# Transposing layer A's normalised rows: from a host-transposed input to one DMA crossbar transfer per group

## The chip, the cores and the metric

The kernel runs on one NeuronCore of a Trainium2 chip. The metric is device time in microseconds (us), from the first to the last instruction and what lies around them. An engine is named PE (TensorE matmul), PEld (TensorE weight load), DVE (VectorE), ACT (ScalarE), POOL (GpSimd) or SP (SyncE, which here issues nearly all DMAs).

## The reference

Input `x` holds 128 graphs of 128 tokens with 384 features, `adj` a 128 x 128 matrix for each. Two layers follow each other, each on layer-normalised rows and each with a residual.

```
x = x + gnn(layernorm(x), adj, adj, Wq, Wk, Wv, bv, Wo, bo)
x = x + ffn(layernorm(x), Wqk, bqk, Wv, bv, conv_w, conv_b, glob, ...)
...
q = (x @ Wq.T).reshape(b, n, 12, 32)          # gnn: layer A
k = (x @ Wk.T).reshape(b, n, 12, 32)
v = (x @ Wv.T + bv).reshape(b, n, 12, 32)
scores = einsum('bqhd,bkhd->bhqk', q, k) * scale + 2 * adj
out = einsum('bhqk,bkhd->bqhd', softmax(scores), v) @ Wo.T + bo
```

Layer A is attention with 12 heads and an additive bias. Layer B (`ffn`) is a causal attention with three experts of width 128, one of which has a convolved query, and a top-2 gate. The change touches layer A alone, and in it the step from `layernorm(x)` to the operand of the products with Wq, Wk and Wv.

## The kernel before, in words

The 128 batches are worked in 32 groups of four (`GB = 4`, `NG = 32`). The matmuls of q, k and v need the normalised rows transposed: features on the partitions, in three chunks of 128 (`KC = 3`), and tokens along the row. They are also wanted in two fp16 parts, a high part and a rest (`a_hT_hi`, `a_hT_lo`), so that three fp16 matmuls (`three_pass`) stand for one fp32 matmul.

The work is cut into steps with names such as `A.qk.0`, and each engine goes through its own written-out list of steps in order: `FIRST_STEPS` (groups 0 and 1), `ORDER_OF_STEPS` (one turn, repeated for 30 turns with groups 2 to 31) and `LAST_STEPS`. In turn t the steps marked `ahead` (`A.hT`, `A.qk`, `A.stack`) work on group t, the other A steps on group t-1 and the B steps on group t-2. An engine that waits in one step holds up all steps behind it in its list. The steps that matter here, for a turn:

- PE: `... B.qk.3 A.mix.0 A.turn.1.0 A.turn.1.1 B.qk.4 B.qk.5 A.score.3.0 B.v.3 A.score.3.1 A.turn.1.2 A.proj.0 A.qk.0 A.mix.1 ...`. `A.qk.0` is the first to read the transposed rows. Each `A.qk` is nine matmuls of 512 columns.
- POOL: `... A.norm.1 A.hx.0 A.hx.1 A.hx.2 A.norm.2 ...`. `A.hx.c` adds the negative mean to chunk c of the transposed x (line 1177).
- DVE: `... A.score.2.2 A.hm.0 B.v.2 A.hm.1 A.hm.2 A.hT.0 A.mix.0 A.smax.2 A.hT.1 A.hT.2 B.v.3 ...`. `A.hm.c` multiplies chunk c by 1/std (line 966), `A.hT.c` writes the low part (line 971).
- ACT: `... A.turn.1.0 A.hT.0 A.mix.0 A.hT.1 A.turn.1.1 A.hT.2 B.qk.4 A.score.2.1 B.qk.5 ...`. `A.hT.c` writes the high part (line 709).
- SP: `A.stat A.rows A.xT A.stack.0 A.res A.adj A.stack.1 B.proj.0 ...`. `A.stat` stores a group's means and 1/std to DRAM, `A.rows` loads them back broadcast over all partitions (`stat_wide`), `A.xT` loads the next group's x, which the host has laid out transposed (`xt`). `A.stack.0` and `A.stack.1` then copy q and k within SBUF in 12 transfers of 96 KB each, for the scores of the next turn.

Groups 0 and 1 do without the host-transposed input. There POOL (and DVE for two batches of group 0, the step `W.share`) normalises rows token-major (`h1`), PE transposes them through PSUM (line 589), and ACT and DVE split what lies in PSUM.

Of the kernel before, what the change touches and what calls it, by code (L numbers as in the profile page):

```python
# [35 lines left out]
P = 128  # L36
# [17 lines left out]
H1_POOL = 2  # L54
# [34 lines left out]
        A.hT.0@0 W.turn.0@0 W.spread.0@0 A.hT.1@0 A.hT.2@0 W.warm.1@0 A.qk.0@0 A.qk.1@0 W.turn.1@0 A.qk.2@0  # L89
        A.qk.3@0 W.spread.1@0 A.qk.4@0 A.qk.5@0 W.turn.2@0 A.v.0@0 W.spread.2@0 W.warm.0@0 A.score.0.0@0  # L90
        A.score.0.1@0 A.score.0.2@0 A.v.1@0 A.v.2@0 A.score.1.0@0 A.score.1.1@0 A.v.3@0 A.hT.0@1 A.score.1.2@0
        A.turn.0.0@0 A.turn.0.1@0 A.score.2.0@0 A.hT.1@1 A.hT.2@1 A.turn.0.2@0 A.score.2.1@0 A.score.2.2@0
        A.qk.0@1 A.mix.0@0 A.turn.1.0@0 A.qk.1@1 A.turn.1.1@0 A.score.3.0@0 A.score.3.1@0 A.turn.1.2@0 A.qk.2@1
        A.score.3.2@0 A.qk.3@1 A.mix.1@0 A.turn.2.0@0 A.qk.4@1 A.turn.2.1@0 A.qk.5@1 A.turn.2.2@0 A.proj.0@0
        A.proj.1@0 A.mix.2@0 A.turn.3.0@0 A.turn.3.1@0 A.turn.3.2@0 A.proj.2@0 A.mix.3@0 A.proj.3@0
    """,
    "act": """
        A.hT.0@0 W.hi.0@0 A.hT.1@0 W.hi.1@0 A.hT.2@0 W.sum.5@0 W.sum.4@0 A.qk.0@0 A.qk.1@0 W.sum.3@0 A.qk.2@0
        A.qk.3@0 W.sum.6@0 A.qk.4@0 A.qk.5@0 W.hi.2@0 W.stack.1@0 A.score.0.0@0 A.score.0.1@0 A.score.0.2@0
        W.hi.3@0 A.hT.0@1 A.score.1.0@0 W.hi.4@0 A.score.1.1@0 A.score.1.2@0 A.hT.1@1 A.turn.0.0@0 W.hi.5@0  # L100
        A.turn.0.1@0 A.hT.2@1 A.score.2.0@0 A.turn.0.2@0 W.hi.6@0 A.score.2.1@0 A.mix.0@0 A.qk.0@1 A.turn.1.0@0
        A.qk.1@1 A.turn.1.1@0 W.hi.7@0 A.turn.1.2@0 A.score.2.2@0 A.qk.2@1 A.score.3.0@0 A.score.3.1@0 A.mix.1@0
        A.qk.3@1 A.turn.2.0@0 A.qk.4@1 A.score.3.2@0 A.turn.2.1@0 A.turn.2.2@0 A.qk.5@1 A.mix.2@0 A.turn.3.0@0
# [42 lines left out]
        A.score.2.2 A.hm.0 B.v.2 A.hm.1 A.hm.2 A.hT.0 A.mix.0 A.smax.2 A.hT.1 A.hT.2 B.v.3 A.score.3.0 A.proj.0  # L146
        A.norm.2 A.score.3.1 A.qk.0 A.mix.1 B.gate.0 B.score.0 A.qk.1 A.score.3.2 B.gate.1 B.score.1 B.gate.2
        B.norm.0 A.qk.2 B.norm.1 A.smax.3 A.norm.3 B.score.2 A.qk.3 B.mix.0 A.proj.1 B.norm.2 B.score.3 B.mix.1
        B.proj.0 A.qk.4 A.mix.2 A.qk.5 B.norm.3 B.proj.1 A.ln2.0 B.mix.2 A.ln2.1 A.proj.2 A.mix.3 A.ln2.2
        B.mix.3 B.proj.2 A.proj.3 A.ln2.3 B.proj.3  # L150
    """,
    "pool": """
        A.res.0 A.ln1 A.res.1 B.res.0 B.res.1 A.norm.0 A.res.2 A.res.3 A.norm.1 A.hx.0 A.hx.1 A.hx.2 A.norm.2
        B.norm.0 B.norm.1 B.res.2 A.norm.3 B.norm.2 B.norm.3 A.ln2.0 B.res.3 A.ln2.1 A.ln2.2 A.ln2.3 A.adj
    """,
    "sp": """
        A.stat A.rows A.xT A.stack.0 A.res A.adj A.stack.1 B.proj.0 B.proj.1 B.proj.2 B.proj.3
# [52 lines left out]
def turned(step, g):  # L210

    return step[:2] == ("A", "hT") and g >= TURNED

# [8 lines left out]
def ahead(step):  # L222
    return step[0] == "A" and step[1] in ("hT", "qk", "stack", "xT", "stat", "rows", "hx", "hm")
# [20 lines left out]
TURNED = 2  # L244
# [11 lines left out]
def build(nc, x, xT, stat_rows, adj, wq, wk, wv, wo, a_bv, a_bo, wqk, bqk, wv2, wg1, wp, b_bv, bg1, wg2, bg2, b_bp,  # L256
          conv_w, conv_b, out):
    with ExitStack() as ctx:
# [178 lines left out]
        def following(g):  # L437
            return g + 1
# [27 lines left out]
        def _(sp):  # L466
# [68 lines left out]
        def _(pe):  # L535
# [17 lines left out]
            def do(step, g, last):  # L553
# [676 lines left out]
```

## Time and profile before

| what | value |
|---|---|
| time, median of 3 runs | 2218.86 us (2217.16 to 2220.27) |
| span of the profiled execution | 2214.1 us |
| what lies around the span, by the median | 4.8 us |
| PE busy | 2167.0 us, 98% |
| DVE busy | 1959.1 us, 88% |
| ACT busy | 1490.3 us, 67% |
| POOL busy | 1198.7 us, 54% |
| mean granted TensorE clock | 0.997 |

The profiled execution has no time of its own beside its span; the median stands for it. Shares of busy time are means over the whole span. Whether a wait costs anything is seen only in the stretch where it lies, so most of the rows further down come from one turn in the middle, between 985 and 1075 us.

### The profile page before, as it was taken

How to read it: one execution, taken by the hardware profiler on the slowest of the kernel's cores; microseconds unless marked ns; L12 is line 12 of the kernel's file. 1: busy time of each engine (PE TensorE's matmuls, PEld its weight loads, DVE VectorE, ACT ScalarE, POOL GpSimd, SP SyncE). 2: the span in 40 equal slices, each digit the busy share in tenths (PEclk: the TensorE clock that was granted, in tenths of full speed). 3: DMA queues.
4: the chain of work that ended last, by engine and by line, in shares of the span. 5: the costliest groups of instructions: out<-in, count | busy, mean ns of one | idle time of the engine just before them, and what ended most of it. 6: DMA issues, size and time to landing. Idle time of an engine off the chain costs nothing.

```text
span 2214.1 us, 51113 instructions
## 1 busy us (share of the span) xinstructions
PE 2167.0 (98%) x16581; PEld 1388.2 (63%) x16581; DVE 1959.1 (88%) x7242; ACT 1490.3 (67%) x5298; POOL 1198.7 (54%) x1521
## 2 busy tenths in 40 slices
PE   5899999999999999999999999999999999999988
PEld 3566666666666666666666666666666666666655
DVE  6889998889988899988899988899988899888984
ACT  4667766677666676666676666677666776666763
POOL 2755565555565545565545665555655555655452
PEclk9999999999999999999999999999999999999999
DMA  5332333332333332333322333322333323333200
GB/s 178 77 93 54 80 90 98 92 84 55 88 87 101 92 77 58 92 87 92 100 69 59 100 87 92 99 52 75 94 94 92 83 59 86 87 101 92 47 27 29
DMA packets 182105, 182.62 MB, mean 82 GB/s; under 512 B 48977, under 2 KB 173521, under 8 KB 181841
## 3 DMA queue, kind: packets, MB, share of 16 engines
q1 hardware_dynamic: 179648, 178.07, 31.1%
q8 instruction: 134, 2.20, 0.5%
q14 instruction: 131, 1.07, 0.3%
q10 hardware_dynamic: 2192, 1.29, 0.2%
HBM read 78.50 MB, written 25.29 MB: 47 GB/s over the span
## 4 chain that ended last, share of the span: by engine, by line
PE 93%; DVE 3%; SPq 1%; ACT 1%; DMA 1%; issue 1%; POOL 0%; DVEq 0%
PE B_bank L546 33%; PE A_bank L546 32%; PE A_bank L626 7%; PE A_bank L638 4%; PE B_bank L620 4%; PE B_bank L645 4%; PE A_bank L613 4%; PE B_bank L630 2%; PE B_bank L589 2%; DVE raw_score L1001 1%; SPq L521 1%; DMA x1res<-in_wqk 1%; DVE smax L1007 0%; DVE V L990 0%; ACT S L755 0%
## 5 line engine op out<-in xcount | busy, mean ns | idle before, releaser
L1147 POOL TENSOR_TENSOR S<-S,rowf 128x512 f32<-128x512 f32 x384 | 414.9, 1108 | 459.9 <-DVE rowf L1026 457.1
L748 ACT ACTIVATE S<-raw_score,smin 128x128 f32<-128x128 f32 x1536 | 595.0, 392 | 94.6 <-DVE smin L1001 94.6
L1001 DVE CUSTOM_DVE_ANT_0 raw_score<-A_bank,adj,s_unit 128x128 f32<-128x128 f32 x1536 | 433.1, 344 | 6.5 <-PE A_bank L613 3.4
L1152 POOL TENSOR_TENSOR S<-S,row2f 128x384 f32<-128x384 f32 x128 | 105.8, 826 | 450.2 <-DVE row2f L1034 447.2
L748 ACT ACTIVATION_READ_ACCUMULATOR S<-raw_score,smin 128x1 f32 x1536 | 293.4, 191 | 0.0
L626 PE MATMUL A_bank<-ident,S 128*128 128x128 f32 x1536 | 218.7, 275 | 5.9 <-POOL S L1147 5.2
L1007 DVE TENSOR_REDUCE smax<-raw_score 128x12 f32<-128x1536 f32 x128 | 222.7, 1740 | 0.0
L762 ACT ACTIVATE PT<-A_bank 128x512 f32<-128x512 f32 x384 | 210.0, 590 | 7.6 <-PE A_bank L626 6.9
L626 PEld LDWEIGHTS A_bank<-ident,S 128*128 128x128 f32 x1536 | 176.5, 141 | 33.2 <-issue 10.4
L713 ACT ACTIVATE b_hT_hi<-B_bank 128x512 f16<-128x512 f32 x96 | 53.2, 588 | 191.1 <-PE B_bank L589 191.1
L762 ACT ACTIVATE PT<-B_bank 128x384 f32<-128x384 f32 x128 | 62.8, 491 | 158.9 <-PE B_bank L630 158.9
L755 ACT ACTIVATE S<-S,s2min 128x128 f32<-128x128 f32 x384 | 148.3, 389 | 3.4 <-DVE s2min L1011 3.4
L613 PE MATMUL A_bank<-Ks,Qs 96*128 96x128 f16 x1536 | 133.5, 219 | 5.6 <-DMA Ks<-k_hi 2.7
L1011 DVE CUSTOM_DVE_ANT_0 S<-B_bank,later 128x128 f32<-128x128 f32 x384 | 90.6, 286 | 53.1 <-PE B_bank L620 52.9
L613 PEld LDWEIGHTS A_bank<-Ks,Qs 96*128 96x128 f16 x1536 | 110.0, 97 | 39.0 <-issue 3.9
L546 PE MATMUL A_bank<-wv_hi,a_hT_hi 128*128 128x384 f16 x384 | 125.7, 327 | 5.9 <-issue 4.9
L546 PE MATMUL B_bank<-wv2g_hi,b_hT_hi 128*128 128x416 f16 x384 | 130.3, 339 | 0.0
L546 PE MATMUL B_bank<-wv2g_hi,b_hT_lo 128*128 128x416 f16 x384 | 130.1, 339 | 0.0
L546 PE MATMUL B_bank<-wv2g_lo,b_hT_hi 128*128 128x416 f16 x384 | 130.1, 339 | 0.0
L546 PE MATMUL A_bank<-wo_hi,oT_hi 128*128 128x384 f16 x384 | 125.2, 326 | 2.6 <-DVE oT_lo L982 2.6
L1133 POOL TENSOR_TENSOR xres<-xin,bo_row 128x384 f32<-128x384 f32 x128 | 127.6, 1008 | 0.0
L546 PE MATMUL B_bank<-wp_hi,yT_hi 128*128 128x384 f16 x384 | 125.5, 327 | 1.3 <-DVE yT_lo L982 1.3
(196 smaller groups left out, 6330.0 us busy)
## 6 DMA issues: line engine op xcount, KB each, us to landing
xin<-in_x SPq DMA_DIRECT2D x32, 768.0 KB, 5.0
Qs<-q_hi SPq DMA_DIRECT2D x256, 96.0 KB, 2.2
out<-x1res SPq DMA_DIRECT2D x128, 192.0 KB, 2.1
Ks<-k_hi SPq DMA_DIRECT2D x252, 96.0 KB, 3.2
xt<-in_xT SPq DMA_DIRECT2D x30, 768.0 KB, 4.2
stat_wide<-stat_rows SPq DMA_DIRECT2D x30, 512.0 KB, 4.4
Qs<-q_lo SPq DMA_DIRECT2D x128, 96.0 KB, 2.2
Ks<-k_lo SPq DMA_DIRECT2D x126, 96.0 KB, 2.9
```

Of the source, the lines that this page charges most:

```text
L546: mm = nc.tensor.matmul(dst, left(c)[a], right(c)[b], start=(c == 0 and n == 0), stop=(c == KC - 1 and n == 2))
L613: mm = nc.tensor.matmul(dst[:, tok(j)], Qs[:, c * HPC + j, tok(b)], Ks[:, c * HPC + j, tok(b)], start=True, stop=True)
L626: mm = nc.tensor.transpose(dst[:, tok(j)], S[b % 2][:, c * HPC + j, :], ident[:])
L748: ins = nc.scalar.activation(S[b % 2][:, h, :], raw_score[:, h, :], ACT.Exp, bias=smin[b % 2][:, h:h + 1], scale=-1.0, accum_out=ssum[b % ...
L755: ins = nc.scalar.activation(S2[b % 2][:, e, :], S2[b % 2][:, e, :], ACT.Exp, bias=s2min[b % 2][:, e:e + 1], scale=-1.0, accum_out=s2sum[b ...
L762: nc.scalar.activation(dst, src[:, 0:dst.shape[1]], ACT.Copy).then_inc(evacuated[stage, "act"], 1)
L1001: ins = nc.vector.tensor_tensor_reduce(raw_score[:, h, :], src[:, j * T:(j + 1) * T], adj2[:, b, :], s_unit[:], 3.0e38, ALU.add, ALU.min, ...
L1007: nc.vector.tensor_reduce(smax[b % 2][:], raw_score[:], AXX, ALU.max).then_inc(maxed, 1)
L1011: ins = nc.vector.tensor_tensor_reduce(S2[b % 2][:, e, :], src[:, e * T:(e + 1) * T], later[:], 1.0, 3.0e38, ALU.add, ALU.min, s2min[b % 2 ...
L1133: nc.gpsimd.tensor_tensor(xres[:, b, :], xin[g % 2][:, b, :], bo_row[:], ALU.add).then_inc(xres_ready, 1)
L1147: nc.gpsimd.tensor_tensor(S[b % 2][:, hs, :], S[b % 2][:, hs, :], rowf[b % 2][:, hs].unsqueeze(2).broadcast_to([P, HPC, T]), ALU.mult).the ...
L1152: nc.gpsimd.tensor_tensor(S2[b % 2][:], S2[b % 2][:], row2f[b % 2][:].unsqueeze(2).broadcast_to([P, NE, T]), ALU.mult).then_inc(normed2, 1)
```

## The change

The host-transposed input `xT`, the DRAM scratch `stat_rows` and the steps `A.stat`, `A.rows`, `A.xT`, `A.hx`, `A.hm` and `W.share` are gone. For every group POOL now normalises each of the four batches token-major (`A.h1.0` to `A.h1.3`, through two buffers of one batch each), ACT and DVE split each batch into its fp16 parts (`A.hT.0` to `A.hT.3`, 128 x 384 each), and SP, once all four batches are split, issues one transposing DMA from `h1_parts` (128 partitions x 3072 fp16, 768 KB) to `h1T`, which holds 24 blocks of 128 x 128. PE's `A.qk.0` waits for the whole transfer. PE's transposes of groups 0 and 1 are gone too. The lists of PE for a steady turn are unchanged; ACT and DVE get a fourth `A.hT` right behind the third.

```diff
-        A.score.2.2 A.hm.0 B.v.2 A.hm.1 A.hm.2 A.hT.0 A.mix.0 A.smax.2 A.hT.1 A.hT.2 B.v.3 A.score.3.0 A.proj.0
...
+        A.score.2.2 B.v.2 A.hT.0 A.mix.0 A.smax.2 A.hT.1 A.hT.2 A.hT.3 B.v.3 A.score.3.0 A.proj.0 A.norm.2
...
-        A.res.0 A.ln1 A.res.1 B.res.0 B.res.1 A.norm.0 A.res.2 A.res.3 A.norm.1 A.hx.0 A.hx.1 A.hx.2 A.norm.2
...
+        A.res.0 A.ln1 A.res.1 B.res.0 B.res.1 A.norm.0 A.res.2 A.res.3 A.norm.1 A.h1.0 A.h1.1 A.h1.2 A.h1.3
...
-        A.stat A.rows A.xT A.stack.0 A.res A.adj A.stack.1 B.proj.0 B.proj.1 B.proj.2 B.proj.3
+        A.hT.0 A.hT.1 A.hT.2 A.hT.3 A.stack.0 A.res A.adj A.stack.1 B.proj.0 B.proj.1 B.proj.2 B.proj.3
...
-        xt = sb("xt", [P, KC, GB * T])
-        h1 = xt[:].rearrange("p c n -> p (c n)").rearrange("p (b n) -> p b n", b=GB)
+        h1 = sb("h1", [P, 2, C])
+        h1_parts = sb("h1_parts", [P, GB, 2, C], F16)
+        h1T = sb("h1T", [P, GB, 2 * KC, T], F16)
...
+                if (stage, kind) == ("A", "hT"):
+
+                    wait_evacuated(sp, step, g)
+                    if b == GB - 1:
+                        if not g == 0:
+                            wait_products(sp, ("A", "v", GB - 1, 0), before(g))
+                            wait_products(sp, ("A", "qk", 2 * KC - 1, 0), before(g))
+                        sp.dma_start_transpose(h1T[:].rearrange("p b n t -> p (b n) t"),
+                                               h1_parts[:].rearrange("p b n c -> p (b n c)")).then_inc(h1_turned, 16)
...
+                if A and kind == "qk" and b == 0:
+                    pe.wait_ge(h1_turned, count(g, 16, 16))
+
+                def columns(c):
+                    return [h1T[:, :, n + c, :] for n in (0, KC)] if A else [h[:, c, :] for h in (hT_hi, hT_lo)]
...
+                    act.wait_ge(h1_ready, count(g, GB, b + 1))
+                    if b == 0 and not g == 0:
+                        act.wait_ge(h1_turned, count(g, 16, 0))
+                    nc.scalar.activation(h1_parts[:, b, 0, :], h1[:, b % 2, :], ACT.Copy, scale=H_SCALE)\
                         .then_inc(hi_ready["ahead"], 1)
...
-            def normed_rows1(g):
+            def normed_rows1(g, b):
                 pool.wait_ge(rstd1_done, count(g, 1, 1))
...
+                if b >= 2:
+                    wait_evacuated(pool, ("A", "hT", b - 2, 0), g)
+                elif not g == 0:
+                    wait_evacuated(pool, ("A", "hT", b + 2, 0), before(g))
+                nc.gpsimd.tensor_scalar(h1[:, b % 2, :], xin[g % 2][:, b, :], stat[g % 2][:, 0, b:b + 1],
+                                        stat[g % 2][:, 1, b:b + 1], ALU.add, ALU.mult).then_inc(h1_ready, 1)
```

The operand that PE streams in `A.qk` was one run of 512 columns and is now four runs of 128 (`columns`).

## Rows read from the trace of the kernel before

**Rows 1.** The page: busy time of each engine.

```profile
PE 2167.0 (98%) x16581; PEld 1388.2 (63%) x16581; DVE 1959.1 (88%) x7242; ACT 1490.3 (67%) x5298; POOL 1198.7 (54%) x1521
```

**Rows 2.** Windows, one turn: length, busy of PE, PEld, DVE, ACT, POOL; clock, DMA.

```profile
1000.00:1067.00 67.00, 67.00 (x519) 43.04 (x517) 60.57 (x226) 45.94 (x166) 37.07 (x47) 1.00 0.33 84
```

**Rows 3.** The chain that ended last, in order of time: start, length, what.

```profile
472.22 9.24 PE A_bank L546 x45
...
1074.93 9.23 PE A_bank L546 x45
```

**Rows 4.** Waits of PE over the span: total, times, longest.

```profile
PE A_bank L546 <- DVE a_hT_lo L971: 2.2, 1, 2.2
```

**Rows 5.** Timeline of a turn, 990 to 1000.1 us: start, length, engine, line.

```profile
990.26 4.19 POOL L1177 TENSOR_TENSOR xt<-xt,stat_wide 128x512 f32<-128x512 f32 x3
...
991.58 1.74 DVE L966 TENSOR_TENSOR xt<-xt,stat_wide 128x512 f32<-128x512 f32 x1
992.00 0.60 ACT L762 ACTIVATE PT<-A_bank 128x512 f32<-128x512 f32 x1 [0.17 <-PE A_bank L626]
...
993.24 0.64 DVE L990 SCALAR_TENSOR_TENSOR V<-B_bank,v_unit,bvg_row 128x416 f32<-128x416 f32 x1
...
993.89 0.47 ACT L766 ACTIVATE oT_hi<-A_bank 128x384 f16<-128x384 f32 x1
...
995.57 0.58 ACT L762 ACTIVATE PT<-A_bank 128x512 f32<-128x512 f32 x1
...
996.13 0.54 DVE L982 TENSOR_TENSOR oT_lo<-A_bank,oT_hi 128x384 f16<-128x384 f32 x1
...
996.60 1.74 DVE L1007 TENSOR_REDUCE smax<-raw_score 128x12 f32<-128x1536 f32 x1
...
998.26 1.28 DVE L971 SCALAR_TENSOR_TENSOR a_hT_lo<-xt,a_hT_hi 128x512 f16<-128x512 f32 x2
...
1000.06 0.38 PE L546 MATMUL A_bank<-a_hT_hi,wq_hi 128*128 128x512 f16 x1
```

**Rows 6.** Groups of instructions: count, busy us and mean ns, idle before.

```profile
L1177 POOL TENSOR_TENSOR xt<-xt,stat_wide 128x512 f32<-128x512 f32 x90 | 126.0, 1427 | 0.0
...
L966 DVE TENSOR_TENSOR xt<-xt,stat_wide 128x512 f32<-128x512 f32 x90 | 106.3, 1207 | 0.0
...
L1165 POOL TENSOR_SCALAR h<-x,nmean,rstd 128x384 f32<-128x384 f32 x128 | 84.6, 661 | 14.0
...
L971 DVE SCALAR_TENSOR_TENSOR a_hT_lo<-xt,a_hT_hi 128x512 f16<-128x512 f32 x90 | 58.6, 677 | 0.0
...
L709 ACT ACTIVATE a_hT_hi<-xt 128x512 f16<-128x512 f32 x90 | 56.4, 627 | 47.2 <-DVE xt L966 47.2
```

**Rows 7.** DMA issues: count, KB each, median us from issue to landing.

```profile
Qs<-q_hi SPq DMA_DIRECT2D x256, 96.0 KB, 2.2
...
xt<-in_xT SPq DMA_DIRECT2D x30, 768.0 KB, 4.2
```

**Rows 8.** SP's own queue in a turn: start, length, what it issued.

```profile
1015.12 5.13 SPq L521 DMA_DIRECT2D Qs<-q_hi  x8
```

**Rows 9.** A long gap of PE at the start (timeline), then windows with the clock.

```profile
33.84 0.27 PE L565 MATMUL B_bank<-ident,wmax 128*2 128x128 f32 x1
39.03 0.39 PE L546 MATMUL A_bank<-wv_hi,a_hT_hi 128*128 128x384 f16 x1 [4.91 <-issue]
...
40.00:42.00 2.00, 2.00 (x8) 0.68 (x6) 1.83 (x8) 0.00 (x0) 1.82 (x3) 0.50 1.13 239
42.00:44.00 2.00, 2.00 (x16) 1.98 (x17) 1.01 (x5) 0.00 (x0) 1.91 (x4) 0.86 0.35 67
```

**Rows 10.** Timeline of groups 0 and 1: low parts, first `A.qk`.

```profile
19.52 1.88 DVE L971 SCALAR_TENSOR_TENSOR a_hT_lo<-A_bank,a_hT_hi 128x512 f16<-128x512 f32 x3
20.35 0.38 PE L546 MATMUL A_bank<-a_hT_hi,wq_hi 128*128 128x512 f16 x1 [2.22 <-DVE a_hT_lo L971]
...
64.61 0.63 PE L546 MATMUL A_bank<-a_hT_hi,wq_hi 128*128 128x512 f16 x1
```

More of the change, by code:

```diff
@@ L53 @@
 GH = 32
-H1_POOL = 2
 VG = C + GH
@@ L96 @@
+        A.turn.0.2@0 A.score.2.1@0 A.score.2.2@0 A.qk.0@1 A.mix.0@0 A.turn.1.0@0 A.qk.1@1 A.turn.1.1@0
+        A.score.3.0@0 A.score.3.1@0 A.turn.1.2@0 A.qk.2@1 A.score.3.2@0 A.qk.3@1 A.mix.1@0 A.turn.2.0@0 A.qk.4@1
+        A.turn.2.1@0 A.qk.5@1 A.turn.2.2@0 A.proj.0@0 A.proj.1@0 A.mix.2@0 A.turn.3.0@0 A.turn.3.1@0
+        A.turn.3.2@0 A.proj.2@0 A.mix.3@0 A.proj.3@0
     """,
     "act": """
-        A.hT.0@0 W.hi.0@0 A.hT.1@0 W.hi.1@0 A.hT.2@0 W.sum.5@0 W.sum.4@0 A.qk.0@0 A.qk.1@0 W.sum.3@0 A.qk.2@0
@@ L99 @@
[L99 to L103, printed above, removed]
@@ L206, with crossed @@
 }
-def turned(step, g):
-    return step[:2] == ("A", "hT") and g >= TURNED
+def crossed(step):
+    return step[:2] == ("A", "hT")
 def parse(word):
@@ L222, in ahead @@
 def ahead(step):
-    return step[0] == "A" and step[1] in ("hT", "qk", "stack", "xT", "stat", "rows", "hx", "hm")
+    return step[0] == "A" and step[1] in ("hT", "qk", "stack", "h1")
 def whole_program(engine):
@@ L691, in do @@
                 A = stage == "A"
-                src = bank_of(step, g) if kind in EVAC and not turned(step, g) else None
+                src = bank_of(step, g) if kind in EVAC and not crossed(step) else None
                 if kind == "hi":
@@ L703, in do @@
                                           k_parts[n % 2][j * HD:(j + 1) * HD, :, :]).then_inc(ks_stacked, 16)
[L704 to L709 removed]
+                elif kind == "hT" and A:
+                    act.wait_ge(h1_ready, count(g, GB, b + 1))
+                    if b == 0 and not g == 0:
+                        act.wait_ge(h1_turned, count(g, 16, 0))
+                    nc.scalar.activation(h1_parts[:, b, 0, :], h1[:, b % 2, :], ACT.Copy, scale=H_SCALE)\
                         .then_inc(hi_ready["ahead"], 1)
@@ L943, in do @@
                 A = stage == "A"
-                src = bank_of(step, g) if kind in EVAC and not turned(step, g) else None
+                src = bank_of(step, g) if kind in EVAC and not crossed(step) else None
                 freed = evacuated[counted(step), "dve"] if stage != "W" else None
@@ L950, in do @@
                         weight_max(b)
-                    elif kind == "share":
-                        h_share()
                     elif kind == "top":
@@ L1117, in _ @@
             statistics1(0)
-            normed_rows1(0)
+            for b in range(GB):
+                normed_rows1(0, b)
             pool.wait_ge(bo_loaded, 16)
```

156 lines of the change are left out of this document (52 added, 104 removed).

## The prediction

> **What bounds the kernel now.** I read the page first. It puts PE at 2167.0 us, 98% of the span, with DVE next at 88% [rows 1]. A share of busy time can hide stretches with other limits, so next come the windows: in a turn of the middle PE is busy for all of its 67.00 us, at full clock, while DVE has 6.4 us free, ACT 21 and POOL 30 [rows 2]. The chain of waits says the same in another way. It runs through PE, and one run of matmuls recurs at 472.22 and, nine turns later, at 1074.93, so a turn takes 602.71 / 9 = 66.97 us [rows 3]. There are 30 such turns, 2009 us of 2214.1. The reader is to see two things. PE's list decides the time, and it has no gap left, so work taken from another engine gives nothing back by itself. And what PE is made to wait for in a turn is paid in full, 30 times. PE's waits today show one single wait for the transposed rows in the whole run, 2.2 us [rows 4].
>
> **What goes.** In a turn POOL loses three additions of 1427 ns (4.3 us) and DVE three multiplications of 1207 ns (3.6 us) [rows 6]. SP loses three DMAs, of which the load of 768 KB is the largest [rows 7]. PE had no part in these steps, and its turn is full: the gain in time is nothing. What it buys is that the split can end sooner.
>
> **What comes on POOL, ACT and DVE.** No group of the trace has the new instructions, so I scale. POOL's normalisation of one batch is the same operation as layer B's, 661 ns: 0.7 us [rows 6]. The high part takes 627 ns for 512 columns, for 384 some 0.5; the low part 677 ns, for 384 some 0.55 [rows 6]. Now I walk the turn with its own times [rows 5]. POOL is free at 990.26, so batches 0 and 1 are normalised by 991.7. ACT is free after the copy that ends at 992.60: high part 0 at 993.10, the output's copy (0.47) 993.57, high part 1 994.07, the next copy (0.58) 994.65. DVE comes to the place of the old multiplications at 991.58, does `B.v.2` (0.64), waits for high part 0 and ends low part 0 at 993.65. `h1` has only two buffers, so here a new wait begins: POOL may make batch 2 only now, and has it at 994.35. DVE goes on with the output's low part (0.54) and the row maximum (1.74) to 995.95, then low part 1 at 996.5 and low part 2 at 997.05. Batch 3 waits for low part 1: POOL 997.2, ACT 997.7, low part 3 ends at 998.25. Behind POOL in this wait stands `A.norm.2`, which is not due before DVE's steps behind `A.hT.3`; behind ACT stands `B.qk.4`, which is copied out about a microsecond later than at present and which PE next asks for after `A.qk.0`. Neither is late if `A.qk.0` waits for longer than that, and about 1 us a turn is what it costs without this cover. Today the last low part ends at 998.26 + 1.28 = 999.54, so the split ends 1.3 us sooner than before.
>
> **What comes on SP and PE.** Before, `A.qk.0` could start on chunk 0 while chunk 2 was on its way. It starts at 1000.06, without idle time ahead of it [rows 5]. Now it wants the whole transfer, issued at 998.25. The slack is 1000.06 - 998.25 = 1.8 us, and with a time D from issue to landing PE stands still for D - 1.8 us in each turn. Nothing is behind `A.qk.0` that PE could do instead. On SP the copies of q and k are queued behind the transfer, but they need `A.qk.2` and `A.qk.5`, which are as late themselves.
>
> D is the unknown of this prediction: the trace has no transposing transfer. The bounds come from the nearest rows. From below, a plain copy of 96 KB within SBUF lands after 2.2 us, and a plain load of the same 768 KB after 4.2 us [rows 7]. From above, the 24 blocks of 128 x 128 could pass one by one: with the 0.64 us that SP takes for each of its eight issues (5.13 / 8) [rows 8], the last lands at 24 x 0.64 + 2.2 = 17.6 us; with 2.2 us for each, at 52.8 us. In between lies the row that is nearest in kind: the eight pieces of the high part of q are also 768 KB from SBUF to SBUF in many short runs, and they take 5.13 us of issue and 2.2 us to land the last [rows 7, 8], 7.3 us. I take 7.3: a transposition should not be quicker than a plain load and needs not be served block by block. PE then waits 7.3 - 1.8 = 5.5 us a turn, 165 us over 30 turns.
>
> **The clock.** PE has had no long gap in mid-run so far. At the start it had one of 4.91 us before 39.03, and the granted clock then was 0.50 up to about 42.4 (0.50 in one window of 2 us, 0.86 in the next) [rows 9], the lower of the two levels, 1.2 GHz. Some 3.4 us of matmuls at half speed are 1.7 us lost. A gap of 5.5 us should do the same in each turn: 51 us. If the clock holds, nothing.
>
> **The operand in four runs.** No row has a matmul that streams four runs of 128. I take nothing, since the operand has as many columns as before; four starts of 2 ns would be 0.4 us a turn over 54 matmuls, 13 us, and that is inside the range.
>
> **The start.** Group 0's low parts end at 21.40 and its first `A.qk` starts at 20.35 [rows 10]. By the same walk batch 3 is split at 22.5, and with 7.3 us the first `A.qk` starts at 29.8, 9.4 us later. For group 1 I find 6 us (64.61 to 70.9). PE has gaps in this stretch anyway [rows 9], so I count 10 of these 16 us, with 0 and 16 as bounds.
>
> **The sum.** 165 + 51 + 10 = 226 us on the span of 2214.1 us: 2440. The median of the runs stands 4.8 us above this span, so 2445 us against 2218.9, 10% slower. Differences under 0.2%, some 4 us, can't be told from no change here.
>
> **Rivals.** Each is a different D, or a different slack.
>
> *As fast as a plain copy.* D is 4.2, the wait 2.4 us a turn: 72 us, and 4 at the start, 2295 us. If the clock falls in these shorter gaps as well, 2346. For it speaks that the DMA engines are busy for 0.33 of a turn only [rows 2], and less without what the change removes; against it, that the rows for short runs are slower than those for long ones. The Trainium skill holds with this rival: "Advanced Engine Details and Errata", section "X-Bar Transpose (TRN2)", says that such transfers are as fast as regular ones, at 350 to 400 GB/s. No run here shows it yet.
>
> *Block by block.* D is 17.6, the wait 15.8 and the clock 1.7, so 525 us over the turns and some 30 at the start: 2774 us; at 2.2 us a block D is 52.8 and the time near 3900. For it speaks that SP's queue issues in pieces and that 24 separate blocks must be written; against it, that it is one instruction with one completion. The Trainium skill has a figure on this side, in "VectorE: DVE Perf Modes", section "The three transpose paths": 1309 ns for one 128 x 128 block of bf16 through the DMA crossbar. By an estimate from it 24 blocks in a row would take 31 us and the sum would be near 3200 us.
>
> *Hidden, and not slower.* If the split ended D before 1000.06, PE would not wait at all. With D = 2.2 the last low part must be done at 997.9 instead of 998.25, and with 4.2 at 995.9, before the row maximum is out of the way. Then the time would be 2219 give or take 3, the start deciding the sign, since the first `A.qk` of groups 0 and 1 has its own wait. It decides from D below 1.8 us. Against it: no copy within SBUF lands that soon.
>
> **How the numbers follow.** The forecast, D from 5.5 to 11 us, gets 0.42 and has a range of its own of 2390 to 2575 us; the plain copy 0.22; block by block 0.27, of which 0.07 lies above 17.6 us of D; hidden 0.07; 0.02 is for what I have not thought of. The range goes from 2290, just under the plain copy, to 2790, just over 17.6 us a transfer, and leaves out the hidden case and the far end of the third. All cases but the hidden one are slower: 0.92. The hidden one is split 0.05 to no difference and 0.03 to faster, because PE's turn itself can't become shorter.
>
> **What the profile after would show.** PE's largest wait should be at `A.qk.0`, released by the transposing DMA, about 32 times, with some 5.5 us each. In the windows of a turn PE should be under 100% busy and its clock under 1.00 behind the gap. DVE's multiplications and POOL's additions should be gone, with the last low part at the same distance from `A.proj.0` as worked out here, 1.8 us ahead of its end. The DMA view should give D. The prediction is wrong if D is far from 7.3 us, if the split is late through the wait for the two buffers (DVE idle before `A.hT.3`), if PE waits for the copies of q and k instead, or if PE does not wait.

## The result and the profile after

The changed kernel takes 2420.2 us (median of four runs, 2419.1 to 2423.2), the kernel before 2218.0 on the same chip (2216.1 to 2220.3): 9.2% slower, a ratio of 1.0916 with an interval of 1.0900 to 1.0931. The predicted 2445 us is 25 us too high. The traces show whether the terms of the sum are as good as their total, so I go through them in the order of the prediction.

The page of the changed kernel, busy time first and then the groups of the matmuls with Wq and Wk (columns: busy us and mean ns of one, then idle time just before):

```profile
PE 2230.8 (92%) x16557; PEld 1402.4 (58%) x16557; DVE 1855.1 (77%) x7182; ACT 1493.0 (62%) x5330; POOL 1159.8 (48%) x1553
...
L535 PE MATMUL A_bank<-h1T,wq_hi 128*128 128x512 f16 x576 | 211.4, 455 | 150.9 <-DMA h1T<-h_parts 150.8
...
L535 PE MATMUL A_bank<-h1T,wk_hi 128*128 128x512 f16 x576 | 171.3, 379 | 0.7 <-DVE smin L979 0.7
```

The matmuls with Wk in the kernel before, for the same comparison:

```profile
L546 PE MATMUL A_bank<-a_hT_hi,wk_hi 128*128 128x512 f16 x288 | 109.2, 379 | 1.0 <-DVE smin L1001 0.7 <-DVE wk_lo L781 0.3
```

Against [rows 1] DVE has 104 us less to do and POOL 39, and PE has 64 us more, with 24 matmuls fewer. The second line names both reasons at once: idle time of 150.8 us that a DMA ended, and 455 ns in the mean for a matmul that takes 379 at full clock (as those with Wk do, which never stand behind a wait).

PE's waits in the changed kernel between 150 and 2300 us, and below them the DMA issues of the transposing transfer and of two plain ones (columns as in [rows 7]):

```profile
PE A_bank L535 <- DMA h1T<-h_parts: 121.7, 30, 4.6
```

```profile
xin<-in_x SPq DMA_DIRECT2D x32, 768.0 KB, 4.9
Qs<-q_hi SPq DMA_DIRECT2D x256, 96.0 KB, 2.2
...
h1T<-h_parts SPq DMA_TRANSPOSE x32, 5.6
```

There is one kind of wait and it comes in every turn: 121.7 / 30 = 4.06 us. The transfer lands 5.6 us after its issue. The timeline shows where these two meet, here in one turn (rows of POOL, ACT and DVE on the split, then SP and PE):

```profile
1017.70 1.31 POOL L1083 TENSOR_SCALAR h<-xin,stat 128x384 f32<-128x384 f32 x2
...
1020.32 0.56 DVE L949 SCALAR_TENSOR_TENSOR h_parts<-h,h_parts 128x384 f16<-128x384 f32 x1 [0.69 <-ACT h_parts L700]
...
1021.05 0.66 POOL L1083 TENSOR_SCALAR h<-xin,stat 128x384 f32<-128x384 f32 x1 [2.04 <-DVE h_parts L949]
1021.26 1.74 DVE L985 TENSOR_REDUCE smax<-raw_score 128x12 f32<-128x1536 f32 x1
...
1022.92 1.01 DVE L949 SCALAR_TENSOR_TENSOR h_parts<-h,h_parts 128x384 f16<-128x384 f32 x2
1023.64 0.83 POOL L1083 TENSOR_SCALAR h<-xin,stat 128x384 f32<-128x384 f32 x1 [1.93 <-DVE h_parts L949]
...
1024.50 0.52 ACT L700 ACTIVATE h_parts<-h 128x384 f16<-128x384 f32 x1 [2.23 <-POOL h L1083]
...
1025.06 0.56 DVE L949 SCALAR_TENSOR_TENSOR h_parts<-h,h_parts 128x384 f16<-128x384 f32 x1 [1.12 <-ACT h_parts L700]
...
1025.82 3.70 SPq L496 DMA_TRANSPOSE h1T<-h_parts  x1
...
1031.51 0.80 PE L535 MATMUL A_bank<-h1T,wq_hi 128*128 128x512 f16 x2 [4.01 <-DMA h1T<-h_parts]
```

The split goes step for step as it was walked: POOL waits twice, 2.04 and 1.93 us, for a low part that frees one of the two `h1` buffers, and the last low part is the end of it. PE is idle from 1031.51 - 4.01 = 1027.50, the transfer is issued at 1025.82: the slack is 1.7 us where the prediction had 1.8.

How long is a turn? The first and the last transfer of the repeated turns, 29 turns apart:

```profile
148.29 3.69 SPq L496 DMA_TRANSPOSE h1T<-h_parts  x1
...
2271.59 3.65 SPq L496 DMA_TRANSPOSE h1T<-h_parts  x1
```

(2271.59 - 148.29) / 29 = 73.22 us, against 66.97 by [rows 3]. Of the 6.25 us more, 4.06 are the wait. The other 2.19 us lie behind it. The windows of two turns of the changed kernel (columns as in [rows 2]; the clock is the third number from the right):

```profile
957.70:960.00 2.30, 2.29 (x6) 0.85 (x7) 0.00 (x0) 0.00 (x0) 1.63 (x2) 0.50 0.00 0
960.00:962.00 2.00, 2.00 (x12) 0.65 (x14) 0.00 (x0) 0.26 (x1) 0.00 (x0) 0.50 0.00 0
962.00:964.00 2.00, 2.00 (x30) 1.57 (x23) 0.96 (x2) 1.13 (x5) 0.00 (x0) 0.63 0.00 0
964.00:966.00 2.00, 2.00 (x14) 1.16 (x14) 1.86 (x8) 1.23 (x7) 0.00 (x0) 1.00 0.04 8
...
1027.50:1031.50 4.00, 0.00 (x1) 0.02 (x1) 2.27 (x13) 2.41 (x10) 1.40 (x2) 1.00 0.93 174
1031.50:1034.00 2.50, 2.49 (x7) 0.97 (x8) 0.00 (x0) 0.00 (x0) 1.64 (x2) 0.55 0.00 0
1034.00:1036.00 2.00, 2.00 (x28) 0.75 (x25) 0.03 (x1) 0.60 (x1) 0.00 (x0) 0.71 0.00 0
1036.00:1038.00 2.00, 2.00 (x18) 1.59 (x15) 1.94 (x6) 1.84 (x9) 0.00 (x0) 1.00 0.06 12
```

PE is empty for 4 us, and behind that the granted clock is at 0.50, that is 1.2 GHz: from the first matmul on in the first of these turns, within about a microsecond in the second. What is lost is the length of each window times one less its clock: 2.5 x 0.45 + 2.0 x 0.29 = 1.7 us in the second turn, and 2.3 x 0.5 + 2.0 x 0.5 + 2.0 x 0.37 = 2.9 us in the first. The turns of the changed kernel are of these two kinds, most of them 72.7 or 73.8 us long.

What is left is the start. The first `A.qk` of groups 0 and 1, and the first matmul of layer B (columns as in [rows 10]):

```profile
29.83 1.03 PE L535 MATMUL A_bank<-h1T,wq_hi 128*128 128x512 f16 x2 [15.33 <-DMA h1T<-h_parts]
...
86.78 1.01 PE L535 MATMUL A_bank<-h1T,wq_hi 128*128 128x512 f16 x2 [13.76 <-DMA h1T<-h_parts]
...
125.38 0.38 PE L535 MATMUL B_bank<-b_hT_hi,wq_hi 128*128 128x512 f16 x1
```

In [rows 10] the first two are at 20.35 and 64.61. The third, in the kernel before:

```profile
105.17 0.38 PE L546 MATMUL B_bank<-b_hT_hi,wq_hi 128*128 128x512 f16 x1
```

So the start costs 125.38 - 105.17 = 20.2 us. The sum of what the trace shows: 30 x 4.06 + 30 x 2.19 + 20.2 = 207.7 us, and the spans differ by 2421.4 - 2214.1 = 207.3.

### The profile page after: what moved, and what is told of

It is laid out like the page before. It is cut to its first block, busy times and chain, and to the rows that moved or that the text cites. A ratio compares the mean times of both kernels' runs of the same rounds, so it can differ in the third digit from the quotient of the medians.

```text
span 2421.4 us, 51141 instructions
## 1 busy us (share of the span) xinstructions
PE 2230.8 (92%) x16557; PEld 1402.4 (58%) x16557; DVE 1855.1 (77%) x7182; ACT 1493.0 (62%) x5330; POOL 1159.8 (48%) x1553
## 2 busy tenths in 40 slices
DMA packets 241593, 168.35 MB, mean 70 GB/s; under 512 B 116144, under 2 KB 240688, under 8 KB 241328
## 3 DMA queue, kind: packets, MB, share of 16 engines
q10 hardware_dynamic: 2192, 1.29, 0.2%
## 4 chain that ended last, share of the span: by engine, by line
PE 77%; DVE 8%; DMA 8%; ACT 3%; issue 2%; POOL 1%; SPq 1%; POOLq 0%; DVEq 0%
PE A_bank L535 30%; PE B_bank L535 23%; DMA h1T<-h_parts 7%; PE A_bank L617 5%; PE A_bank L629 4%; PE B_bank L611 4%; PE B_bank L636 4%; PE A_bank L604 3%; DVE smax L985 3%; DVE h_parts L949 2%; PE B_bank L621 2%; PE B_bank L581 2%; ACT h_parts L700 1%; DVE raw_score L979 1%; POOL h L1083 1%
## 5 line engine op out<-in xcount | busy, mean ns | idle before, releaser
L535 PE MATMUL A_bank<-h1T,wq_hi 128*128 128x512 f16 x576 | 211.4, 455 | 150.9 <-DMA h1T<-h_parts 150.8
L535 PE MATMUL A_bank<-wv_hi,h1T 128*128 128x384 f16 x768 | 199.3, 328 | 5.9 <-DVE wv_lo L772 5.0
L535 PEld LDWEIGHTS A_bank<-h1T,wq_hi 128*128 128x128 f16 x576 | 59.7, 110 | 229.1 <-issue 182.4
L955 DVE SCALAR_TENSOR_TENSOR q_lo<-A_bank,q_hi 128x512 f16<-128x512 f32 x96 | 66.1, 689 | 161.8 <-ACT q_hi L713 160.2
L713 ACT ACTIVATE q_hi<-A_bank 128x512 f16<-128x512 f32 x96 | 57.0, 594 | 214.6 <-PE A_bank L535 214.6
L535 PE MATMUL A_bank<-h1T,wk_hi 128*128 128x512 f16 x576 | 171.3, 379 | 0.7 <-DVE smin L979 0.7
L1083 POOL TENSOR_SCALAR h<-xin,stat 128x384 f32<-128x384 f32 x128 | 89.2, 700 | 128.9 <-DVE h_parts L949 128.7
L535 PE MATMUL A_bank<-h1T,wq_lo 128*128 128x512 f16 x288 | 131.2, 456 | 0.0
```

Of the source, the lines that this page charges most:

```text
L535: mm = nc.tensor.matmul(dst, left(c)[a], right(c)[b], start=(c == 0 and n == 0), stop=(c == KC - 1 and n == 2))
L1083: nc.gpsimd.tensor_scalar(h1[:, b % 2, :], xin[g % 2][:, b, :], stat[g % 2][:, 0, b:b + 1], stat[g % 2][:, 1, b:b + 1], ALU.add, ALU.mult) ...
```

## The experiments

The first theory is that the whole loss is the transfer's time from issue to landing, as far as PE sees it, with the lower clock that follows and with the first two groups' own waits. The rivals: PE streams the four-run operand more slowly; the lower clock belongs to the new work and not to the wait; the split is late whatever the transfer takes; the transfer's size costs nothing. The kernel before takes 2217.6 to 2219.1 us in the three sets of runs, and each ratio is against the runs of its own set.

**1. Take the wait away.** From group 2 on, `A.qk` reads layer B's rows, which lie in one run and are ready; `A.v`, much later in PE's list, waits for the transfer.

```diff
-                if A and kind == "qk" and b == 0:
+                early = A and kind == "qk" and g >= 2
+                if A and (kind == "qk" and b == 0 and g < 2 or kind == "v" and b == 0):
                     pe.wait_ge(h1_turned, count(g, 16, 16))
...
-                    return [h1T[:, :, n + c, :] for n in (0, KC)] if A else [h[:, c, :] for h in (hT_hi, hT_lo)]
+                    return [h1T[:, :, n + c, :] for n in (0, KC)] if A and not early else [h[:, c, :] for h in (hT_hi, hT_lo)]
```

> From group 2 on the query and key products read layer B's transposed rows instead of the crossbar's, which are there long before, so TensorE waits for the transfer only at the value products of the next turn; the split and the transfer stay as they are, and the queries and keys are those of other rows. Theory 1 (a turn loses 4.06 us to the wait at the first query product and some 2.1 us to the clock behind it, nothing to the split): turns of 66.97 us as before, only the later start of some 20 us is left, 2238 us (2228 to 2250), clock 1.00 in the turns. Theory 2 (the token-major split in four pieces with its waits between POOL, ACT and DVE slows the turn itself): above 2300 us, turns of 69 us or more without any wait for the transfer.

Measured: 2247.2 us (ratio 1.0130, 1.0115 to 1.0145), inside the range of theory 1. 173 of the 202 us are gone, with the split, the transfers and their 24 blocks all still there, so theory 2 falls. A turn (columns as in [rows 2]):

```profile
1000.00:1067.30 67.30, 67.26 (x518) 42.97 (x516) 57.55 (x224) 46.05 (x168) 35.77 (x49) 1.00 0.35 76
```

The turn is 67.3 us, 0.3 to 0.4 us longer than before. Laid beside a turn of before, PE's rows fall behind by 0.39 us at `B.score.0` and `A.turn.2.0`, and there ACT's last copy for layer B ends 0.6 us after the first `A.qk` has started, where it ended 0.5 us ahead of it before. Of the remaining 29 us 20 lie at the start (the first matmul of layer B is again at 125.38), and 0.3 us or so in each of 30 turns make up the rest. This run can't acquit the four-run operand, which it takes out too.

**2. Keep PE at work in the wait.** 18 matmuls of 512 columns on a weight tile, into the bank that `A.qk.0` overwrites, ahead of the wait.

```diff
                     pe.wait_ge(h1_turned, count(g, 16, 16))
+                    for _ in range(18 if g > 0 else 0):
+                        nc.tensor.matmul(dst[:, :], WQ[0][:, 0, 0:P],
+                                         WQ[0][:].rearrange("p c n -> p (c n)")[:, 0:4 * P], start=True, stop=True)
```

> Eighteen matmuls of 512 columns on weights, into the bank that the first query product then overwrites, are put ahead of the wait from group 1 on: 18 x 0.2155 = 3.9 us of work that fits in the wait of 4.06 us. Theory 1: the wait ends at the same time, the granted clock stays at 1.00 behind it, and the 2.1 us a turn come back: 2420 - 30 x 2.1 = 2357 us (2345 to 2375). Theory 3 (the slow stretch behind the wait is not due to the idle time, but to the operand in four runs or to the crossbar's data): the clock still falls and the time stays at 2415 to 2430 us.

Measured: 2361.5 us (1.0649, 1.0632 to 1.0667), inside the range of theory 1, and 59 us faster than the changed kernel for 558 more matmuls. Theory 3 falls. The windows over the stretch that was the wait, and right behind it:

```profile
1002.90:1007.00 4.10, 4.06 (x20) 1.67 (x18) 2.27 (x13) 2.59 (x10) 1.32 (x2) 1.00 0.96 180
1007.00:1011.00 4.00, 4.00 (x43) 2.55 (x44) 1.19 (x3) 1.62 (x5) 1.72 (x2) 1.00 0.00 0
```

PE can't be at its real work any sooner, and yet the clock stays at 1.00 and the turn falls from 73.22 to 71.10 us. So 2.1 us a turn, some 60 us, are the price of the clock alone, and it is the empty stretch that brings it, not the new work. The four-run operand costs nothing: behind these matmuls the nine of `A.qk.0` are through in 2.05 us, where the kernel before takes 2.03, and those with Wk take 379 ns in the mean in both.

**3. One transfer per batch.** Four transfers of 192 KB, each issued when its batch is split.

```diff
-                    if b == GB - 1:
...
-                        sp.dma_start_transpose(h1T[:].rearrange("p b n t -> p (b n) t"),
-                                               h1_parts[:].rearrange("p b n c -> p (b n c)")).then_inc(h1_turned, 16)
+                    sp.dma_start_transpose(h1T[:, b, :, :],
+                                           h1_parts[:, b, :, :].rearrange("p n c -> p (n c)")).then_inc(h1_turned, 16)
...
```

> Four transfers of 192 KB, each issued when its batch is split, instead of one. Theory 4a (the 5.6 us are 0.15 us of SP's queue for each of the 24 blocks and some 2 us to land the last): only six blocks are left after the last split, 0.9 + 2.0 = 2.9 us instead of 5.6, so the wait falls from 4.06 to 1.4 us and the time to 2340 us if the clock still falls, 2285 if not. Theory 4b (a fixed cost for each transfer, whatever its size): each lands after 5 us or more, the wait stays at 4 us or grows, 2420 us or more.

Measured: 2286.5 us (1.0307, 1.0292 to 1.0323). DMA issues, and PE's waits between 150 and 2090 us:

```profile
h1T<-h_parts SPq DMA_TRANSPOSE x128, 2.9
```

```profile
PE A_bank L534 <- DMA h1T<-h_parts: 46.7, 28, 2.3
```

Only the last batch's 2.9 us stand in PE's way, 1.67 us a turn, and most turns are 68.65 us long: the wait and nothing else. Theory 4a holds, with its time for a clock that does not fall; 4b falls. Two thirds of the loss go with one edit on SP and the counts that PE and ACT wait for.

**4. Split earlier.** Four `h1` buffers (two lists of small tiles are packed into one tensor to make room), POOL's `A.h1` ahead of `A.norm.1`, ACT's `A.hT` ahead of `A.score.2.0`, DVE's four `A.hT` together behind `B.v.2`. One transfer as in the change.

```diff
-        A.score.2.2 B.v.2 A.hT.0 A.mix.0 A.smax.2 A.hT.1 A.hT.2 A.hT.3 B.v.3 A.score.3.0 A.proj.0 A.norm.2
+        A.score.2.2 B.v.2 A.hT.0 A.hT.1 A.hT.2 A.hT.3 A.mix.0 A.smax.2 B.v.3 A.score.3.0 A.proj.0 A.norm.2
...
-        h1 = sb("h1", [P, 2, C])
+        h1 = sb("h1", [P, GB, C])
...
```

> Four one-batch buffers instead of two, the normalisation ahead of POOL's second softmax scaling, the high parts in ACT's idle time ahead of the third score step, and the low parts behind one another ahead of the third row maximum: by the times of the changed kernel's turn the last low part ends 3.8 us sooner, at 1021.95 instead of 1025.75. Theory 1: the transfer lands at 1027.5 where TensorE comes to it at 1027.35, the wait is 0.2 us, the clock stays up: 2245 us (2230 to 2265), the later start being left. Theory 2 (the split itself costs): no better than 2350 us, because the moved work holds up the scores.

Measured: 2242.6 us (1.0111, 1.0096 to 1.0126), inside the range of theory 1. PE's waits between 150 and 2090 us:

```profile
PE A_bank L536 <- DMA h1T<-h_parts: 4.4, 4, 1.9
```

PE waits for the transfer four times only, and most turns are 67.16 us long. So the transfer of 768 KB can be hidden. What stays is mostly at the start, where the two waits are 14.2 and 13.8 us and the first matmul of layer B comes 19.1 us later than before.

**5. Group 1's steps moved forward** in the list of the first turns, on top of run 4. POOL's list is shown; those of ACT and DVE are changed alike.

```diff
-        A.res.0@0 A.ln1@0 A.h1.0@1 A.h1.1@1 W.adj.0@0 A.res.1@0 A.res.2@0 A.norm.0@0 A.h1.2@1 A.res.3@0 W.lo.4@0
-        A.norm.1@0 A.h1.3@1 W.lo.5@0 W.lo.6@0 A.norm.2@0 W.lo.7@0 A.norm.3@0 A.adj@0 A.ln2.0@0 A.ln2.1@0
+        A.res.0@0 A.ln1@0 A.h1.0@1 A.h1.1@1 W.adj.0@0 A.h1.2@1 A.h1.3@1 A.res.1@0 A.res.2@0 A.norm.0@0 A.res.3@0 W.lo.4@0
+        A.norm.1@0 W.lo.5@0 W.lo.6@0 A.norm.2@0 W.lo.7@0 A.norm.3@0 A.adj@0 A.ln2.0@0 A.ln2.1@0
...
```

> The early split (four h1 buffers, steps moved forward) and in addition, in the written-out list of the first turns, group 1's normalisation and split are moved ahead of group 0's A.norm.1. The whole computation is done. Theory 1 (what the early split still cost above the kernel before, 2242.6 against 2217.9, lies mostly in the 13.8 us for which PE waits for group 1's transfer at 83.9 us, because POOL's fourth batch stands behind A.norm.1): that wait falls under 3 us, the 14 us wait of group 0 stays, and the time is 2230 us, 2222 to 2238. Theory 2 (PE lacks other work in this stretch anyway, and the gap only moves to another wait): 2240 us or more.

Measured: 2237.0 us (1.0083, 1.0069 to 1.0097), inside the range of theory 1, but by half of what it promised. The second of the two waits:

```profile
79.74 0.58 PE L536 MATMUL A_bank<-h1T,wq_hi 128*128 128x512 f16 x1 [5.97 <-DMA h1T<-h_parts]
```

Group 1 starts 4.1 us sooner than in run 4 (83.86), not 11, and 6.0 us of wait stay. 3.3 us have turned up as a new wait of PE for DVE's `V`. Theory 2 has part of the truth: work is short in this stretch.

**6. A plain copy of the same 768 KB**, to see what the transposition adds to a copy of that size.

```diff
-                        sp.dma_start_transpose(h1T[:].rearrange("p b n t -> p (b n) t"),
-                                               h1_parts[:].rearrange("p b n c -> p (b n c)")).then_inc(h1_turned, 16)
+                        sp.dma_start(h1T[:].rearrange("p b n t -> p (b n t)"),
+                                     h1_parts[:].rearrange("p b n c -> p (b n c)")).then_inc(h1_turned, 16)
```

> The transposing transfer is replaced by a plain copy of the same 768 KB from h1_parts to h1T, rows of 6 KB on each partition, one DMA. So the rows are not transposed and the products of layer A are computed from the wrong operand; all instructions on the engines are the same. Theory 1 (a plain copy of that size is quicker than the crossbar's 5.6 us from issue to landing: 4.2 us or less, as the plain load of 768 KB of the kernel before, or as two copies of 96 KB at 2.2 us): PE's wait falls from 4.1 us to 2.7 us a turn or less, and the time is 2375 us, 2330 to 2390. Theory 2 (the crossbar moves the data as fast as a plain copy, and what is paid is the size): landing 5.6 us and 2420 us, 2412 to 2428.

Measured: 2319.9 us (1.0464, 1.0448 to 1.0480). Its DMA issues, then the windows around the ends of two turns that follow each other:

```profile
h1T<-h_parts SPq DMA_DIRECT2D x32, 768.0 KB, 3.6
```

```profile
982.60:984.70 2.10, 0.04 (x2) 0.04 (x2) 0.70 (x3) 2.10 (x10) 0.00 (x0) 1.00 0.69 281
984.70:988.00 3.30, 3.30 (x21) 1.44 (x25) 1.57 (x11) 0.83 (x2) 2.76 (x3) 0.69 0.00 0
988.00:991.00 3.00, 3.00 (x34) 2.22 (x27) 2.12 (x7) 2.13 (x10) 0.27 (x1) 0.77 0.03 8
...
1053.30:1055.40 2.10, 0.03 (x2) 0.04 (x2) 0.71 (x3) 2.10 (x10) 0.00 (x0) 1.00 0.69 281
1055.40:1059.00 3.60, 3.60 (x40) 2.15 (x41) 2.37 (x13) 1.57 (x4) 3.04 (x3) 1.00 0.02 5
```

Theory 1 holds in kind and theory 2 falls: a plain copy lands 2.0 us sooner than the transposing transfer. The time is 10 us below its range. Its 2375 us fit a wait of 2.7 us and a lower clock in every turn; the wait is 2.1 us. The same wait of 2.1 us is followed by a lower clock in one turn (3.3 x 0.31 + 3.0 x 0.23 = 1.7 us lost) and by none in the next, and the turns go 69.1 and 70.7 us by turns.

The traces also show what the two kinds move while the data flow. A window of 1 us in the middle of a transfer, first of the changed kernel (the last number is GB/s):

```profile
1028.50:1029.50 1.00, 0.00 (x0) 0.00 (x0) 0.00 (x0) 1.00 (x7) 0.00 (x0) 1.00 1.16 218
```

And of this run:

```profile
982.60:983.60 1.00, 0.03 (x1) 0.00 (x0) 0.70 (x2) 1.00 (x4) 0.00 (x0) 1.00 1.05 436
```

The transposing transfer runs at half the rate of the plain copy. 786432 bytes take 3.6 us at 218 GB/s and 1.8 us at 436, so in both kinds some 2 us of the time to landing are left in which little or nothing is moved. The two differ in one more thing: the changed kernel moves 116144 packets under 512 B, this run 17328, and the difference is 3088 for each transfer. Whether the crossbar or the short packets halve the rate, no run separates.

**7. Four buffers alone**, in the order of the change (with the packing of run 4, to make room).

```diff
-        h1 = sb("h1", [P, 2, C])
+        h1 = sb("h1", [P, GB, C])
...
-                if b >= 2:
-                    wait_evacuated(pool, ("A", "hT", b - 2, 0), g)
-                elif not g == 0:
-                    wait_evacuated(pool, ("A", "hT", b + 2, 0), before(g))
+                if not g == 0:
+                    wait_evacuated(pool, ("A", "hT", b, 0), before(g))
...
```

> The changed kernel with four h1 buffers in place of two and nothing else changed (the order of all steps as it is). The whole computation is done. Theory 1 (the wait of POOL for the low part of batch 1 delays the last low part, which then ends about a microsecond sooner, and PE's wait shrinks by as much): PE's wait falls from 4.1 to about 3 us a turn and the time is 2385 us, 2370 to 2405. Theory 2 (the row maximum and the output's low part in DVE's list set the last low part, the two buffers only fill idle time): 2420 us, 2412 to 2428.

Measured: 2367.1 us (1.0667, 1.0653 to 1.0682). PE's waits between 150 and 2090 us:

```profile
PE A_bank L536 <- DMA h1T<-h_parts: 80.0, 28, 3.4
```

2.86 us a turn in place of 4.06: the two-buffer wait put 1.2 us on the path, and theory 2 falls. The time is 3 us below the range of theory 1: 53 us are gained, 17 more than the 30 x 1.2 of the waits, since the clock is low for a shorter stretch too: most turns are 71.5 us, 1.7 above the wait and the turn of before.

**8. Runs 5 and 3 together**: early split, new order of the start, one transfer per batch.

> The kernel with the early split and the new order of the first turns, and with one transfer of 192 KB for each batch in place of one of 768 KB. The whole computation is done. Theory 1 (all that the change costs is the exposed time of the transfer, in the turns and at the start, so with both made short the kernel is near the one before): PE's wait at the first A.qk of groups 0 and 1 shrinks by some 2.5 us each and the time is 2225 us, 2217 to 2232. Theory 2 (four issues on SP of 1.3 us each in place of one of 3.7 us delay the copies of q and k, for which PE then waits in each turn): 2240 us or more, with PE's waits for Qs or Ks. Faster than the kernel before: not expected by either, since PE's list is unchanged.

Measured: 2231.0 us (1.0059, 1.0046 to 1.0071), inside the range of theory 1. The window over a turn, to be read against [rows 2]:

```profile
1000.00:1066.90 66.90, 66.90 (x518) 43.00 (x517) 57.30 (x224) 45.88 (x168) 35.49 (x48) 1.00 0.32 76
```

In this turn nothing is lost any more and, with DVE 3 us less busy, nothing is gained; over the turns between 150 and 2070 us the waits for the transfer sum to 4.5 us. PE has no wait for `Qs` or `Ks` in this stretch, so theory 2 falls. The first matmul of layer B is at 117.49 us, 12.3 us later than before, and the time is 11.9 us longer.

**9. Group 0's split ahead of the weights' split**, and a few loads behind its transfers, on top of run 8.

```diff
-        W.max.0@0 W.max.1@0 W.top.0@0 W.scale.0@0 W.max.2@0 W.lo.0@0 A.hT.0@0 A.hT.1@0 A.hT.2@0
-        A.hT.3@0 W.max.7@0 W.unit.0@0 A.qk.0@0 W.lo.1@0 A.qk.1@0 A.qk.2@0 W.top.1@0 W.scale.1@0 W.unit.1@0
+        W.max.0@0 W.max.1@0 W.top.0@0 W.scale.0@0 A.hT.0@0 A.hT.1@0 A.hT.2@0 A.hT.3@0 W.max.2@0 W.lo.0@0
+        W.max.7@0 W.unit.0@0 A.qk.0@0 W.lo.1@0 A.qk.1@0 A.qk.2@0 W.top.1@0 W.scale.1@0 W.unit.1@0
...
```

> As the kernel with the early split and one transfer per batch, and in addition the first group's split stands ahead of the splitting of the weights in the lists of ACT and DVE, and SP issues the loads of Wp and of four bias rows behind the first group's transfers. The whole computation is done. Theory 1 (in the turns nothing is left to lose, at a turn of 66.9 us in the run of that kernel against 66.97 before; what is left, 2231.0 against 2219.1, lies at the start, where the first A.qk of group 0 starts at 29.2 us instead of 20.35): the first A.qk starts at about 22 us and the time is 2224 us, 2219 to 2228. Theory 2 (the first transfers share the DMA engines with the loads of the weights, or the weights' parts come later by as much, so the first A.qk stays at 27 us or more): 2229 us or more.

Measured: 2229.0 us (1.0050, 1.0038 to 1.0063). SP's queue and PE's first `A.qk`:

```profile
14.98 10.32 SPq L494 DMA_TRANSPOSE h1T<-h_parts  x4
...
26.91 1.03 PE L537 MATMUL A_bank<-h1T,wq_hi 128*128 128x512 f16 x2 [11.99 <-DMA h1T<-h_parts]
```

The first transfer is issued 5.6 us sooner than in run 8 (20.56), but the four hold SP for 10.3 us instead of 7.0, and `A.qk.0` gains 2.3 us only. The time is above the range of theory 1, and the numbers lie on the border of theory 2. That the transfers share the DMA engines with the loads of the weights fits this, but no run separates the two.

**10. Two transfers of 384 KB**, to see if the landing time is a line in the number of blocks.

```diff
-                    if b == GB - 1:
...
+                    if b % 2 == 1:
+                        sp.dma_start_transpose(h1T[:, b - 1:b + 1].rearrange("p b n t -> p (b n) t"),
+                                               h1_parts[:, b - 1:b + 1].rearrange("p b n c -> p (b n c)"))\
+                            .then_inc(h1_turned, 16)
...
```

> The changed kernel with two transfers of 384 KB (batches 0 and 1, batches 2 and 3) in place of one of 768 KB, the order of all steps as it is, two h1 buffers. The whole computation is done. Theory 1 (from 5.6 us for 24 blocks and 2.9 us for 6 blocks: a fixed part of 2.0 us and 0.15 us for each block of 128 x 128): landing 3.8 us, PE's wait 2.3 to 3.0 us a turn, clock under 1.00 behind it in some turns only, and 2345 us, 2315 to 2365. Theory 2 (a transfer's duration isn't a line in its blocks, or the second transfer is served only when the first is done, so that it lands as late as one of 768 KB): landing of the second 4.6 us or more and 2385 us or more.

Measured: 2325.9 us (1.0483, 1.0467 to 1.0499), inside the range of theory 1. Its DMA issues, and PE's waits between 150 and 2090 us:

```profile
h1T<-h_parts SPq DMA_TRANSPOSE x64, 3.8
```

```profile
PE A_bank L536 <- DMA h1T<-h_parts: 56.1, 27, 2.3
```

PE waits for 2.1 us a turn, a little under the 2.3 us of theory 1, and most turns go 69.1 and 70.8 us by turns, as in run 6. The landing is 3.8 us, as the line through 2.9 us (6 blocks) and 5.6 us (24 blocks) has it: 2.0 us and 0.15 us for each block of 128 x 128.

No version beats the kernel before. Run 8 shows why the turns give nothing more with this list of PE: it is as full without the wait as it was.

## Why the prediction was right, point by point

**The mechanism** was right: PE's list sets the time, the transfer stands between the last low part and `A.qk.0`, PE has nothing else to do, and the clock falls behind the gap. Run 1 shows that the wait and the clock are the loss of the turns, run 2 separates the two.

**What goes gains nothing**: right. DVE's 104 us and POOL's 39 left no trace in the time; run 8 has them gone and the turn of before.

**The slack** was right: 1.7 us against 1.8. The walk also held in its parts (POOL 700 ns, the high part 520, the low part 570 by the groups of instructions, against 0.7, 0.5 and 0.55). What it didn't say is that 1.2 us of slack were lost to the two buffers (run 7); it counted that wait in its path without pricing it. One of its own signs of being wrong, DVE idle before `A.hT.3`, is there, with 1.12 us, but as part of the path that was walked.

**D was mis-sized**: 5.6 us, not 7.3. The nearest row in kind was eight issues of SP and a landing, but the change makes one issue. Together with the slack this makes 122 us of wait where 165 stood. The bounds were right only because they were wide: the lower one, 4.2 us from a load out of DRAM, lies above the 3.6 us that run 6 measured for a copy within SBUF. As a rival, "as fast as a plain copy" is refuted: 5.6 us against the 3.6 of run 6, or 218 GB/s against 436 while the data move. The Trainium skill says the same as that rival ("Advanced Engine Details and Errata", section "X-Bar Transpose (TRN2)": as fast as regular DMAs, 350 to 400 GB/s). This trace differs from it: 218 GB/s in the middle of a transfer, and 140 from issue to landing (786432 bytes in 5.6 us). "Block by block" is refuted at its prices, for the transfer lands after 5.6 us and not after 17.6 or 52.8. That the blocks pass one behind the other is not refuted: each further block of a transfer adds 0.15 us (run 10), and 32 KB in 0.15 us are the same 218 GB/s. The Trainium skill's 1309 ns for one block ("VectorE: DVE Perf Modes", section "The three transpose paths") is no price for a further block in a transfer, where the runs show 150 ns.

**The clock** was right in kind and a little small: 2.19 us a turn in place of 1.7, 66 us in place of 51. The 1.7 was read from one stretch of [rows 9] and holds for about half of the turns; in the others the clock stays low for some 5.5 us and costs 2.9.

**The operand in four runs** was right at nothing: 379 ns for the matmuls with Wk, before and after.

**The cover of ACT's late copy** was right in kind: uncovered it costs 0.3 to 0.4 us a turn (run 1), not the "about 1 us".

**The start was the worst step**: 20 us, not 10. Group 0 came to the microsecond (29.83 against 29.8), partly by luck, since the issue was at 24.14 and not at 22.5 and the landing took less. For group 1 the prediction names 6 us and shows no walk. The list of the first turns is not that of a turn: `A.h1.3@1` stands behind `A.norm.1@0` there, and its row on POOL starts at 78.65, so the transfer is issued at 81.12 us and lands at 86.7 instead of 70.9. "PE has gaps in this stretch anyway" took off 6 us more, and that discount was too large: group 1's first `A.qk` is 86.78 - 64.61 = 22.2 us late and layer B's first matmul 20.2, so the gaps give back 2 us.

The errors are -43, +15 and +10 us. They add up to -18 of the -19 us by which the span came out below the sum. The other 6 us between 2445 and 2420.2 are two times 3: what lies around the span is 1.8 us in every run with both numbers on record (2423.24 against 2421.4 in the profiled one), not 4.8, and the profiled run is 3.0 us above the median. So the total was better than its terms, and that part is luck. In the chances, the 0.05 and 0.03 into which the hidden case is split make 0.08, where it had been given 0.07; nothing rests on that.

## What to carry to other kernels

When a producer is replaced by a DMA, don't ask what the engines save but when the last piece is issued, how long it takes to land, and what the first consumer has ahead of it in its list. Everything beyond that slack is paid in each turn, and the lower clock behind the gap can add half as much again. Two cures keep the transfer: cut the transfer so that only the last piece is exposed (2420 to 2286 us), and move the producing steps forward and give them buffers of their own (2420 to 2243 us). Walk the start by its own list.

## What the runs showed of the hardware

- A transposing transfer within SBUF lands after 2.9, 3.8 and 5.6 us for 6, 12 and 24 blocks of 128 x 128 in fp16: 2.0 us and 0.15 us a block. A plain copy of the 768 KB lands after 3.6 us. In the middle of the transfer the first moves 218 GB/s and the second 436.
- SP itself is held by the transposing transfer, in the median for 1.29 us with 6 blocks, 1.46 with 12 and 3.66 with 24, against 0.53 us for the plain copy. From 12 to 24 it grows far more than from 6 to 12; why is open.
- How much clock a gap of PE costs in this kernel: nothing in most turns with a gap of 1.6 us (run 3), 1.7 us in every other turn with 2.1 us (runs 6 and 10), 1.7 us in most turns with 2.8 us (run 7), and 1.7 or 2.9 us in each with 4.0 us. Filled with 18 matmuls, the gap of 4.0 us costs none (run 2). Of two gaps alike, one may be followed by the lower level and the next not.
